# Composing the second feed-forward factor during attention, with one output bank for the value products

## The reference, cut to what matters

```python
w = softmax(top_k(logits, 32))
W1 = einsum('k,kir,kro->io', w1, fc1_A, fc1_B)     # fc1_A 32x128x64, fc1_B 32x64x512 -> 128x512
W2 = einsum('k,kir,kro->io', w2, fc2_A, fc2_B)     # fc2_A 32x512x64, fc2_B 32x64x128 -> 512x128
x = x + gelu(layernorm(x) @ W1) @ W2
```

```python
Q, K, V = layernorm(x) @ Wq, ... # 16 heads, two maps of depth 8 each, values of depth 16
attn = softmax(Q1 K1 / sqrt(8), causal) - lam * softmax(Q2 K2 / sqrt(8), causal)
x = x + rms_norm(attn @ V) * rms_scale * 0.2 @ Wo
```

## Time and profile before

| | us |
|---|---|
| median of 3 runs | 428.15 (424.87 to 428.99) |
| the profiled execution | 431.64 |
| its span, first to last instruction | 429.9 |

### The profile page before, as it was taken

One profiled execution on the slowest core, in us unless ns is written; L12 is line 12 of the kernel. 1 busy time (PEld: TensorE's weight loads), 2 busy tenths in 40 slices (PEclk: granted clock), 3 DMA queues, 4 the chain that ended last, 5 costly groups with the idle time before them and its releaser, 6 DMA issues.

```text
span 429.9 us, 9985 instructions
## 1 busy us (share of the span) xinstructions
PE 367.9 (86%) x3316; PEld 236.1 (55%) x3316; DVE 308.9 (72%) x989; ACT 237.0 (55%) x582; POOL 198.4 (46%) x319
## 2 busy tenths in 40 slices
PE   0599697097999898998999898899989989999995
PEld 0466486085555554655554555444866656664774
DVE  5596855079899888897979796864665789998110
ACT  3332521003688778787878686762856244353822
POOL 6223422001558667575758584840016557883000
PEclk9999979569899999999999999969999999999999
DMA  7879998990133313132223200000000000000001
GB/s 207 269 244 309 219 244 243 214 200 10 46 96 88 79 46 83 41 86 57 77 77 76 77 4 5 2 3 2 0 2 0 2 0 0 2 1 0 26 25 50
DMA packets 48930, 34.50 MB, mean 80 GB/s; under 512 B 20080, under 2 KB 43760, under 8 KB 48880
## 3 DMA queue, kind: packets, MB, share of 16 engines
q1 hardware_dynamic: 48880, 33.86, 32.0%
HBM read 25.20 MB, written 8.39 MB: 78 GB/s over the span
## 4 chain that ended last, share of the span: by engine, by line
PE 46%; DVE 19%; SPq 10%; issue 10%; ACT 5%; DMA 4%; POOL 4%; DVEq 0%; POOLq 0%; ACTq 0%
PE ps L1373 6%; PE ps L1164 6%; PE ps L1364 5%; PE ps L1088 5%; SPq L402 3%; PE ps L1096 3%; DVE arena L1506 3%; SPq L430 2%; PE ps L1083 2%; DVE arena L1519 2%; PE ps L1577 2%; PE ps L1168 2%; DVE arena L1025 2%; ACT arena L832 2%; PE ps L1240 2%
## 5 line engine op out<-in xcount | busy, mean ns | idle before, releaser
L784 POOL TENSOR_SCALAR_AFFINE_SELECT arena<-arena 128x256 f32<-128x256 f32 (+1 forms) x192 | 90.1, 484 | 94.5 <-ACT arena L832 90.5
L832 ACT ACTIVATE arena<-ps 128x512 f32<-128x512 f32 x192 | 109.3, 603 | 27.9 <-PE ps L1122 27.7
L1025 DVE TENSOR_REDUCE arena<-ps 128x4 f32<-128x1024 f32 x64 | 78.3, 1223 | 13.0 <-PE ps L1096 10.0
L1018 DVE CUSTOM_DVE_ANT_0 ps<-ps,future 128x128 f32<-128x128 f32 x256 | 66.2, 320 | 10.5 <-PE ps L1083 10.5
L1447 POOL TENSOR_TENSOR arena<-arena 128x1024 f32<-128x1024 f32 x16 | 34.1, 2133 | 40.3 <-DVE arena L1532 40.3
L1122 PE MATMUL ps<-stacks 50*128 50x256 bf16 x256 | 50.6, 278 | 0.3 <-ACT arena L832 0.2
L1088 PE MATMUL ps<-stacks 48*128 48x256 bf16 x256 | 40.8, 276 | 2.2 <-DVE arena L1025 1.9
L1164 PE MATMUL ps<-arena,values 128*17 128x256 f32 x512 | 40.9, 392 | 0.0
L475 POOL TENSOR_TENSOR qk_parts_sb<-qk_rest,qk_parts_sb 128x512 bf16<-128x512 f32 x16 | 19.1, 1211 | 42.1 <-DVE qk_parts_sb L559 42.1
L1018 DVE DVE_READ_ACCUMULATOR2_ANT arena<- 128x1 f32 x256 | 36.1, 141 | 0.0
L1577 PE MATMUL ps<-arena,upto 128*128 128x384 f32 x96 | 35.9, 486 | 0.0
(11 more groups left out here) (140 smaller groups left out, 715.8 us busy)
## 6 DMA issues: line engine op xcount, KB each, us to landing
stacks<-qk_parts SPq DMA_DIRECT2D x96, 128.0 KB, 3.3
qk_parts<-qk_parts_sb SPq DMA_DIRECT2D x16, 384.0 KB, 4.9
arena<-in_L_ffn_fc_B_dram SPq DMA_DIRECT2D x4, 1024.0 KB, 7.9
arena<-in_L_ffn_fc_A_dram SPq DMA_DIRECT2D x16, 256.0 KB, 5.8
xs<-in_L_attn_a_X_dram SPq DMA_DIRECT2D x4, 256.0 KB, 4.0
qk_parts<-qk_parts_sb SPq DMA_DIRECT2D x8, 128.0 KB, 5.3
arena<-in_L_ffn_fc_B_dram SPq DMA_DIRECT2D x4, 256.0 KB, 5.0
stacks<-arena SPq DMA_DIRECT2D x64, 4.0 KB
```

The lines of the kernel that those rows point to most:

```text
L784: nc.gpsimd.affine_select(out=diag, in_=diag, compare_op=ALU.is_ge, fill=0.0, base=0, pattern=[[0, 2 if s < 2 else UMAPS], [1, P]], channe ...
L832: nc.scalar.activation(probs[:, r, s, :], ps[:, bank, :], ACT.Exp, scale=SCALE).then_inc(exp_done, 1)
L1018: last = nc.vector.tensor_tensor_reduce(out=block, in0=block, in1=future[:], scale=1.0, scalar=LOWEST, op0=ALU.add, op1=ALU.max, accum_out ...
L1025: nc.vector.tensor_reduce(out=rowmax[:, gs, 1, UMAPS * uu:UMAPS * (uu + 1)], in_=ps[:, S_BANK + 1:S_BANK + 3, :].rearrange("p b (m k) -> p ...
```

## The change

1. The second factor's products leave the projection stage and the first attention slots. PE does chunk 0's four products at the end of slot 2, and then one product at the end of each slot from 3 to 62. DVE transposes chunk 0 at the end of slot 1, chunk 1 in slot 2, and then one chunk in every fourth slot (6, 10, ... 58). ACT scales fc2_B in slot 1 and copies the sum to `w2` in slot 62.
2. fc2_B and the first quarter of fc2_A are loaded behind the stores of sequence 7. The other three quarters are loaded in pieces of two transfers, one behind the first shift store and one behind each of the stack loads of the groups 4 to 8 (`g` from 0 to 4). fc2's tiles get room of their own in SBUF for that.
3. The products accumulate in bank 6 (`W_BANK`). The value products keep bank 5 alone, so that PE waits for the copy of unit n-1 before it writes unit n.
4. The feed-forward layer's down projection waits for `w2`; the shifted scores of unit 0 no longer do.

```diff
-            load_fc2_a(2)
-            load_fc2_a(3)
+            load_fc2_b(sp)
+            load_fc2_a(sp, 0)
...
+            load_fc2_a(sp, 1, (0, 2))
...
                     load_stack(sp, g + 4, k)
+                    if g < 5:
+                        load_fc2_a(sp, (g + 3) // 2, (0, 2) if g % 2 == 1 else (1, 3))
...
-        S_BANK, T_BANK, O_BANK, M_BANK = 0, 3, 5, 7
+        S_BANK, T_BANK, O_BANK, W_BANK, M_BANK = 0, 3, 5, 6, 7
...
+        def turned_chunk(slot):
+            if slot in (1, 2):
+                return slot - 1
+            c = (slot + 2) // 4
+            return c if (slot + 2) % 4 == 0 and 2 <= c < KR else None
+        def second_products(slot):
+            if slot == 2:
+                return [(0, j) for j in range(FCH)]
+            c = (slot + 1) // 4
+            return [(c, (slot + 1) % 4)] if 1 <= c < KR else []
...
-                    if past(n - 1):
-                        pe.wait_ge(ot_copied, n - 1)
+                    if past(n):
+                        pe.wait_ge(ot_copied, n)
...
             def head(slot):        # ACT
-                if slot == HEAD_SLOTS - 1:
+                if slot == 1:
+                    scale_second_factor(act)
+                if slot == SECOND_END:
...
             def head(slot):        # DVE
+                c = turned_chunk(slot)
+                if c is not None:
+                    turn_factor(dve, c)
...
             def head(slot):        # PE
-                if slot < HEAD_SLOTS:
-                    factors_tensor(pe, SEQS + slot)
+                for c, j in second_products(slot):
+                    if c == 0 and j == 0:
+                        pe.wait_ge(b2_scaled, KR // 2)
+                    pe.wait_ge(fT_done, 4 + c + 1)
+                    product = nc.tensor.matmul(ps[:, W_BANK, j * P:(j + 1) * P], a2T[:, c % 4, j * P:(j + 1) * P],
+                                               b2[:, c, :], start=(c == 0 and j == 0),
+                                               stop=(c == KR - 1), skip_group_check=True)
```

More of the change, by code:

```diff
@@ L185, in hybrid_kernel @@
         late_end = at
+        a2, at = carve(late_end, (KR // 2, F // BLK, R))
+        b2, at = carve(at, (KR, D))
         def part_of(u, side, part):
@@ L317, in scale_factors, with turn_factor @@
             for i in FACTORS[slot][0]:
[L318 to L330, removed]
+                dve.wait_ge(fT_ps, i + 1)
+                nc.vector.tensor_tensor(
+                    a1T[:, 4 * i:4 * i + 4, :],
+                    ps[:, FT_BANK + i % 2, :].rearrange("p (c d) -> p c d", c=4),
+                    mix_col[:, 4 * i:4 * i + 4].unsqueeze(2).to_broadcast([P, 4, P]),
+                    op=ALU.mult).then_inc(fT_done, 1)
+        def turn_factor(dve, n):
             dve.wait_ge(fc2_a_in[n // 4], 16 * P // BLK)
-            dve.wait_ge(acc_done, max(4, i - 3))
+            dve.wait_ge(acc_done, max(4, n + 1))
             nc.vector.transpose(a2T[:, n % 4, :].rearrange("p (j b) -> p j b", b=BLK),
@@ L355, in factor_products @@
             def factor_products(i):
[L356 to L360, removed]
+                pe.wait_ge(fc1_b_in[i], 16)
                 pe.wait_ge(fT_done, i + 1)
                 for j in range(4):
[L363 to L372, removed]
+                    c = 4 * i + j
+                    last = nc.tensor.matmul(ps[:, ACC_BANK, :], a1T[:, c, :], b1[:, c, :],
+                                            start=(c == 0), stop=(c == KR - 1))
                 last.then_inc(acc_done, 1)
@@ L378, in factors_tensor, with load_fc2_a, load_fc2_b @@
                     factor_products(behind[n])
-                if n < len(ahead) and ahead[n] < 4:
+                if n < len(ahead):
                     factor_transposes(ahead[n])
+        def load_fc2_a(sp, quarter, blocks=(0, 2, 1, 3)):
+            for i in blocks:
+                k = PRIMS * BLK // P * i + 2 * quarter
+                sp.dma_start(a2[BLK * i:BLK * (i + 1), 2 * quarter:2 * quarter + 2]
+                             .rearrange("p c j r -> p (c j) r"),
+                             fc2_A[k:k + 2].rearrange("k (j p) r -> p (k j) r", p=BLK))\
+                  .then_inc(fc2_a_in[quarter], 16)
+        def load_fc2_b(sp):
+            for i in (0, 2, 1, 3):
+                k = PRIMS * BLK // P
+                sp.dma_start(b2[BLK * i:BLK * (i + 1)],
+                             fc2_B[k * i:k * (i + 1)].rearrange("k (e p) f -> p (k e) f", p=BLK))\
+                  .then_inc(fc2_b_in, 16)
         def project_sync(sp):
@@ L396, in load_fc1_b @@
                   .then_inc(fc1_b_in[quarter], 16)
[L398 to L412, removed]
             load_fc1_b(0)
@@ L707, in turns @@
                     emit(it, j)
-                    if it == 0 and j <= HEAD_SLOTS:
-                        head(j)
+                    head(SLOTS * it + j)
             for j in range(L_STAT - UPS + 1):
@@ L849, in emit @@
                         act.wait_ge(ott_done, n - 1)
-                    nc.scalar.copy(ot_sb[:, r, :], ps[:, O_BANK + r, 0:SEQ]).then_inc(ot_copied, 1)
+                    nc.scalar.copy(ot_sb[:, r, :], ps[:, O_BANK, 0:SEQ]).then_inc(ot_copied, 1)
                 n = unit(it, j, L_OT)
@@ L1052, in head @@
             def head(slot):
-                if slot < HEAD_SLOTS:
[L1054 to L1057, removed]
+                if slot == 0:
+                    dve.wait_ge(fT_done, 4)
+                    nc.vector.memset(ps[:, O_BANK, 0:SEQ], 0.0).then_inc(cleared, 1)
+                c = turned_chunk(slot)
+                if c is not None:
+                    turn_factor(dve, c)
             turns(dve, emit, amid, head)
@@ L1163, in weigh_values @@
                     if t == 0:
-                        nc.tensor.matmul(ps[32 * m:32 * m + DV + 1, O_BANK + r, 0:SEQ], values[:, tile, head, :],
+                        nc.tensor.matmul(ps[32 * m:32 * m + DV + 1, O_BANK, 0:SEQ], values[:, tile, head, :],
                                          probs[:, p, m // 2, m % 2 * SEQ:m % 2 * SEQ + SEQ],
@@ L1167, in weigh_values @@
                     else:
-                        last = nc.tensor.matmul(ps[32 * m:32 * m + DV + 1, O_BANK + r, P:SEQ],
+                        last = nc.tensor.matmul(ps[32 * m:32 * m + DV + 1, O_BANK, P:SEQ],
                                                 values[:, tile, head, :], probs[:, p, 2, m * P:(m + 1) * P],
@@ L1244, in head @@
             def head(slot):
-                if slot < HEAD_SLOTS:
-                    factors_tensor(pe, SEQS + slot)
+                for c, j in second_products(slot):
[5 more added lines that the diff above has]
+                                               stop=(c == KR - 1), skip_group_check=True)
+                    if j == FCH - 1:
+                        product.then_inc(acc_done, 1)
             turns(pe, emit, amid, head)
@@ L1787, in amid_attend @@
                         pe.wait_ge(ot_copied, UNITS)
+                        pe.wait_ge(w12_done, 2)
                         feed_down_tensor(pe, F1, 0)
```

25 lines of the change are left out of this document (7 added, 18 removed).

## The result

| | before | after |
|---|---|---|
| median of four runs, us | 427.08 (424.87 to 428.99) | 436.4 (435.83 to 438.14) |
| profiled execution, us | 431.64 | 435.87 |
| its span | 429.9 | 434.1 |
| mean granted clock in it | 0.959 | 0.948 |
| slot 6 starts | 102.82 | 96.98 |

The changed kernel is **slower**, by some 2%: ratio 1.021, 95% interval 1.0166 to 1.0254. The forecast was 433.6, slower.

The account below looks back on a forecast made before the run. The prediction took transfers to bound the head and tight handoffs between PE, DVE and ACT the attention. Its terms, -9.5 + 9.4 + 2 + 2.4 + 0.8 + 0.4 = +5.5, gave 433.6 us for the median, range 424 to 441.

Parts of the forecast that it names:

- head, to slot 6 (to slot 8): Head: slot 6 starts at 93.3 instead of 102.82, -9.5 us (ends -14.3 and -3.9).
- one bank: Attention: value products wait for the copy of the unit before, a loop of 2.67 us per slot; +9.4 us in all.
- transposes and loads: Attention: fourteen transposes in DVE's list, +2 us, and fc2_A loads behind the stack loads, +0.8 us.
- products: Attention: one product per slot end, mostly hidden in PE's wait for the copy, exposed once in eight; +2.4 us.
- tail: After the attention: the tail pays one copy, +0.4 us.
- the round of 25 us: Attention, expected sign: eight slots take 25 us instead of 23.1.
- three signs of being wrong: Eight slots under 24 us; slot 1's wait ending before 77; PE waiting for shift stores over 1 us per group, slots 12 to 30.
- The estimate of 16 us: Attention: the bank's cost if each of 56 slots lost the 0.29 us overlap; not adopted, as rows let some slots off.
- 65.6 + 2.0 + 3.8 + 3.8 + 5.8 = 81.0: Head: POOL's end, sequence 7's stores, fc2_B, fc2_A's first quarter and landing; last load lands at 81.0 instead of 84.98.
- the late shift stores: Attention, rival: shift stores queue behind new loads, five groups lose up to 2 us each, 443 us; chance 0.11.
- faster: Attention, rival: the copy wait is absorbed by PE's wait for DVE's large maximum, 419 to 424 us; chance 0.13.
- little difference: Rival: load lands at 78 and the clock recovers soon, or transposes and products find cover; 428 to 431 us; chance 0.26.

Follow-up runs that it names:

- experiment 1: The kernel before with value products on one output bank, waiting for the copy of the unit before, nothing else changed: 438.07 us, ratio 1.0288.
- experiment 3: The changed kernel without the second factor's products of chunks 1 to 15, transposes and loads kept: 435.12 us, ratio to before 1.0212.
- Experiment 4: The changed kernel with fc2_B loaded behind sequence 3's stores and fc2_A's first quarter behind sequence 4's: 425.38 us, ratio to before 0.9962.
- experiment 2: The changed kernel with two output banks again, the second factor's products in their unused halves (sum not right): 431.38 us, ratio to before 1.0124.
- The sixth kernel: The fifth kernel with the first shift store put ahead of the load of stack 3 in the SP queue: 422.22 us, ratio 0.9851.
- the fifth: The changed kernel with earlier loads, the composition done by slot 32 and two output banks from unit 27 on: 421.2 us, ratio 0.9834.

## Why the prediction was right, and which of its sizes were not

The two effects it put first, and their signs, are what the runs show, and the time lies in its range. Read by position, in the profiled executions:

| step | forecast | measured | from |
|---|---|---|---|
| head, to slot 6 (to slot 8) | -9.5 | -5.8 (-4.9) | slot starts |
| one bank | +9.4 | +10.9 | experiment 1, slots 8 to 63 |
| transposes and loads | +2.8 | -0.3 | experiment 3 less 1, 168.33 - 168.63 |
| products | +2.4 | +1.3 | after less experiment 3, 169.63 - 168.33 |
| tail | +0.4 | -2.7 | slot 63 to the end |
| sum, with the head to slot 8 | +5.5 | +4.2 | profiled executions |

That the sum comes so near is luck in part: head and bank together were put 6.1 us too low, the other three 7.3 too high. Between the medians the step is +9.3 us (interval 7.1 to 10.8), which +5.5 does not reach. Of the signs that it set, the round of 25 us and the 0.1 us behind the copy came; slot 6 near 93 and a wait that ends near 81 did not. None of its three signs of being wrong came.

**The bank.** Mechanism right, down to the rows. The loop was put at 2.67 us from the rows of before; after, the second scores of two plain slots are 2.70 apart (208.15 to 210.85). Where the sum let slots off, it was a little too generous: rounds grew by 1.70 and not by 1.4. It held slot by slot: in experiment 1 the second scores of slots 39 to 47 are 3.02, 2.71, 2.71, 2.71, 3.03, 3.11, 2.71 and 4.81 apart, growths of 0.37, 0.26, 0.28, 0.38, -0.27, 0.43, 0.28 and 0 over the earlier trace rows, where the sum had 0.39, 0.22, 0.24, 0.34, -0.4, 0.38, 0.25 and 0. The estimate of 16 us, a lost overlap of 0.29 in every slot, was too high: 10.9 lies nearer to the 9.4 from rows. The Trainium skill's "PSUM — Partial Sum Buffer", section "Summary: rules for kernel authors", says to read PSUM in another bank than a running matmul writes; it gives no price, and experiment 1 agrees with its direction.

**The head.** The step that failed is "65.6 + 2.0 + 3.8 + 3.8 + 5.8 = 81.0". The 65.6 was sound (POOL ended at 64.95), but SP wasn't free: stack 1 stands ahead of sequence 7's stores in its list and was issued from 64.18 to 68.40, so the stores began 2.8 late. The sum left that term out, though its rows had the sign of it: before, POOL ended at 68.6 and the stores began at 73.73. Then stores and fc2_B took 5.1 instead of 5.8, the three issues of fc2_A ahead of the last 5.2 instead of 3.8, and the last landed 6.5 after its issue began (78.77 to 85.31) instead of 5.8: 81.0 + 2.8 - 0.7 + 1.4 + 0.7 = 85.2, against 85.33 measured. This is also past the 85 that it held for the latest possible. So having fewer loads ahead of it gained nothing, where the forecast had 4.0 from that. The rest to slot 6 was put at 12.3 and took 11.65; it was 17.84 before, and the whole gain comes from it. Experiment 4 shows the other side: without that queue slot 6 comes 12.8 us earlier.

**Transposes and products.** The transposes were priced against the tight DVE of before. There they do cost something: 0.76 per round for transposes, products and loads with two banks. But the edit itself made the loop the bound, and in experiment 3 the transposes beside a loop of 2.7 us cost nothing. For the products the sum did see this cover in plain slots, and still put them 1.1 too high. It should have priced both after the bank, not beside it.

**Loads during attention, the late shift stores.** After the change no round after slot 16 differs by over 0.05 us, with loads (slots 9 to 27) or without, and in the list of waits PE's matmuls wait for no shift store (a weight load once, 0.4). So this rival had nothing to bite on there: half a quarter was through in time. The last packet of the last such load ended at 166.26 and the shift store's first moved at 166.34, 1.3 us after its issue began, as in the next group, which has no load ahead of it. With two banks, where slots are shorter, it is closer: in experiment 2 slots 16 to 23 took 24.63, 0.8 over the later rounds, and nearly all of it is slot 18, where PE stood 0.67 us for something that the profile doesn't name; slot 18 reads a shift store. The Trainium skill's "DMA: Bandwidth & Descriptors", section "Queues, rings and completion order", says that an engine takes a queue's descriptors in ring order. The sixth kernel agrees: with six transfers ahead of it, no packet of the store moved in 3.02 us.

**The baseline.** The sum was made against a profiled execution 4.6 us above its median, with the median's distance taken as constant. It isn't. Before, the mean granted clock goes roughly with the time: 0.980 in the run of 422.99 and 0.974 in that of 427.22 (both among the 13 of the experiments), 0.959 in the profiled one. At two levels, 1.2 and 2.4 GHz, 0.959 of 429.9 us is about 35 us at the lower one and 0.974 about 22. Part of it is a stretch of 6.9 us in the tail (281.9 to 288.8) that the profile after lacks. The tail's -2.7 is about what such a stretch costs in the other profiles (last section), so it is no gain of the change. The changed kernel's four runs are all at 0.944 to 0.948. The medians differ by 9.3 us where the profiles differ by 4.2. How much of the remaining 5.1 is the clock no run here separates.

The rivals: *faster* fell because 2.70 is over DVE's 2.44; *little difference* needed a landing at 78, and it was 85.3. Its other leg, cover for transposes and products, did come true (+1.0 instead of the +4.4 of the sum), but the head fell 3.7 short of its -9.5 and the bank cost 1.5 more.

## What to carry to other kernels

When a buffer goes from two copies to one, write down the loop that now closes (reader's end, release, writer, the work behind it back to the reader) and compare it with the slot: here 2.70 us against plain slots of 2.33 to 2.45. Price all other added work after that, against the new bound, since idle time that one edit makes can hide the next. And when a load is moved in a queue, list everything that stands ahead of it at the moment of its release, not only the stores it was put behind. If a bank must be borrowed, borrow it briefly: half the slots with double the work in them gave back more than it cost.

## What was not expected of the hardware

- **The clock stays low long after PE is busy again.** After the change PE stood idle from 70.7 to 86.2 us; the granted clock was 0.50, the 1.2 GHz level, from 64.5 to 105.4. In the windows shown PE was busy 8.73 of 10 us from 90 to 100 us and still at 0.50. Before, PE stood idle from 73.6 to 85.8, and the clock was at 0.50 from 77.1 to 94.2 and for 3.4 us more from 107.9. In experiment 4 it was 0.50 from 66.5 to 93.8, with PE busy 8.26 of 10 us from 80 on.
- **A low stretch in the tail comes and goes.** In the profiles without one (the changed kernel, experiment 2, the sixth) the time from slot 63 to the end is 161.6, 162.3 and 161.6; with 6.8 or 6.9 us of it (before, experiment 1, the fifth) 164.4, 164.1 and 163.9; with 10.2 or 10.3 (experiments 3 and 4) 165.6 both times. So in these profiles some 7 us at half the clock go with about 2.5 us more, and a whole kernel's comparison by profile moves by that much. What sets the stretch isn't known.
- **Issues stretch.** The four transfers of fc2_A's first quarter took 6.64 us to issue beside full DMA engines (share 1.24 from 73.54 to 80.18); in experiment 4 two of another quarter took 1.04 us at 82.91, where the share was 0.04.
